# The input's part of the GRU gates: from two steps a product to a block a product

## The reference

```python
# x (16, 256, 512), initial state cond_2048 (16, 512), W_ih and W_hh (512, 1536)
def cell(h, x):
    gi = x @ W_ih + b_ih
    gh = h @ W_hh + b_hh
    i_r, i_z, i_n = jnp.split(gi, 3, axis=-1)
    h_r, h_z, h_n = jnp.split(gh, 3, axis=-1)
    r = jax.nn.sigmoid(i_r + h_r)
    z = jax.nn.sigmoid(i_z + h_z)
    n = jnp.tanh(i_n + r * h_n)
    h_new = (1.0 - z) * n + z * h
    return (h_new, h_new)
# hs: all 256 states; router: softmax of hs / |hs| @ router_w, the best two of eight, renormalised
for e in range(8):
    out = out + combine[:, e, None] * (hs @ Wa[e] @ Wb[e])     # ranks 128
return x + out
```

## Time and profile before

| | us |
|---|---|
| median of 3 runs (lowest, highest) | 1058.17 (1055.62, 1063.12) |
| the profiled execution | 1050.81 |
| its span, first to last instruction | 1048.9 |
| PE busy | 1001.5 |
| DVE busy | 856.9 |
| ACT busy | 722.4 |
| POOL busy | 298.0 |
| TensorE's granted clock, share of full speed | 0.995 |

### The profile page before, as it was taken

One profiled execution on the slowest core, in us unless ns is written; L12 is line 12 of the kernel. 1 busy time (PEld: TensorE's weight loads), 2 busy tenths in 40 slices (PEclk: granted clock), 3 DMA queues, 4 the chain that ended last, 5 costly groups with the idle time before them and its releaser, 6 DMA issues.

```text
span 1048.9 us, 71107 instructions
## 1 busy us (share of the span) xinstructions
PE 1001.5 (95%) x30225; PEld 860.6 (82%) x30225; DVE 856.9 (82%) x3215; ACT 722.4 (69%) x2824; POOL 298.0 (28%) x762
## 2 busy tenths in 40 slices
PE   4779999999999999999999999999999999999997
PEld 3678888888888888888888888878888888888874
DVE  6888888887887887888888888878888888788886
ACT  7677666776766776766667767767766767676663
POOL 2033223322232322232322233332223332222223
PEclk9899999999999999999999999999999999999999
DMA  8230111111111111111111111111111111110001
GB/s 289 88 90 20 29 30 32 26 31 29 30 32 29 25 32 30 30 31 29 29 28 29 30 32 32 27 28 30 28 33 33 28 28 33 27 29 20 14 5 32
DMA packets 49537, 39.48 MB, mean 38 GB/s; under 512 B 34676, under 2 KB 39112, under 8 KB 49224
## 3 DMA queue, kind: packets, MB, share of 16 engines
q1 hardware_dynamic: 48376, 31.41, 11.3%
q10 hardware_dynamic: 848, 3.54, 1.0%
HBM read 18.94 MB, written 8.39 MB: 26 GB/s over the span
## 4 chain that ended last, share of the span: by engine, by line
PE 90%; DVE 4%; issue 2%; ACT 2%; DMA 1%; ACTq 0%; DVEq 0%
PE obank L1043 16%; PE pairs L898 15%; PE gates L971 13%; PE gates L976 10%; PE nbank L1032 8%; PE ybank L1032 8%; PE nbank L925 7%; PE gates L988 5%; PE gates L984 5%; DMA wih<-in_L_cond_W_ih 1%; PE ybank L1010 1%; DVE tr L777 1%; DVE pre L780 1%; ACT nn L637 1%; DVE pre L786 0%
## 5 line engine op out<-in xcount | busy, mean ns | idle before, releaser
L1043 PE MATMUL obank<-wb,y 128*32 128x512 f16 (+1 forms) x2559 | 209.7, 380 | 4.6 <-issue 4.3
L898 PE MATMUL pairs<-wx,xs 128*32 128x256 f16 x6144 | 195.4, 273 | 5.3 <-issue 5.2
L465 POOL TENSOR_TENSOR y<-y 128x128 f16<-128x128 f32 x256 | 112.1, 438 | 306.6 <-ACT y L673 196.7
L777 DVE STREAM_TRANSPOSE tr<-gates 128x256 f32<-128x256 f32 x256 | 115.0, 449 | 76.9 <-PE gates L976 76.2
L971 PE MATMUL gates<-whh,st 128*32 128x256 f16 x4080 | 163.4, 275 | 14.4 <-DVE st L803 14.2
L629 ACT ACTIVATE rr<-pre 128x64 f32<-128x64 f32 x256 | 65.7, 257 | 158.8 <-DVE pre L780 158.3
L898 PEld LDWEIGHTS pairs<-wx,xs 128*32 128x32 f16 x6144 | 159.4, 97 | 12.0 <-issue 9.0
L976 PE MATMUL gates<-whh,hparts 128*32 128x256 f16 x4080 | 161.3, 273 | 0.4 <-issue 0.3
L971 PEld LDWEIGHTS gates<-whh,st 128*32 128x32 f16 x4080 | 96.6, 96 | 64.3 <-issue 47.1
L830 DVE SCALAR_TENSOR_TENSOR acc<-obank,comb,acc 128x512 f32<-128x512 f32 x186 | 138.4, 744 | 5.3 <-PE obank L1043 4.6
L1043 PEld LDWEIGHTS obank<-wb,y 128*32 128x32 f16 (+1 forms) x2559 | 82.8, 97 | 60.0 <-issue 12.1
(11 more groups left out here) (130 smaller groups left out, 1858.0 us busy)
## 6 DMA issues: line engine op xcount, KB each, us to landing
out<-outb SPq DMA_DIRECT2D x63, 128.0 KB
xin<-in_x SPq DMA_DIRECT2D x58, 128.0 KB
wih<-in_L_cond_W_ih ACTq DMA_DIRECT2D x4, 768.0 KB, 7.6
whh<-in_L_cond_W_hh SPq DMA_DIRECT2D x4, 768.0 KB, 12.1
wih<-in_L_ffn_Wb SPq DMA_DIRECT2D x8, 256.0 KB, 2.7
xs<-xh SPq DMA_TRANSPOSE x116, 3.2
wih<-in_L_ffn_Wa SPq DMA_DIRECT2D x4, 256.0 KB, 4.5
whh<-in_L_ffn_Wa SPq DMA_DIRECT2D x4, 256.0 KB, 3.6
```

The costliest lines, as they stand in the source:

```text
L465: nc.gpsimd.tensor_tensor(y[:, m % YB, 1, :], y32[:, :], y[:, m % YB, 0, :], ALU.subtract).then_inc(ylo_ready, 1)
L777: nc.vector.transpose(tr[:, 0:2 * K, :].rearrange("p (g k) c -> p g k c", k=K), g[:, 0:2 * P].rearrange("p (g c k) -> p g k c", g=2, k=K)) ...
L898: mm = nc.tensor.matmul(bank[32 * j:32 * j + 32, P:3 * P], turned(b, k, ph)[:, t0:t0 + 2 * B], wx[:, pw, k, j, :], start=False, stop=(k == ...
L1043: mm = nc.tensor.matmul(o_at(m)[rows * j:rows * j + rows, :], y[:, m % YB, ph, rows * j:rows * j + rows], wb[:, pw, m % NE, :], start=(ter ...
```

## The change

The input's part of r and z is computed for a whole block: its 128 rows are stationary in four tiles of 32 columns, `wx` of two column groups is moved, 512 columns a matmul, 12 terms for each of two halves (24 x 4 matmuls a block, a quarter of them on each even step, one block ahead). The product has its rows by step: partition 16t + b is step t of the block. `copy_gates` on ACT copies a half to SBUF (`gate_rows`), and `move_gates` on SP moves, for each step, the 16 rows of each of the four column groups by a small DMA (16 rows of 256 f32, 1 KB a row) to the rows 32j to 32j+15 of one of four slots `gate_in`. The rows 32j+16 to 32j+31 of these slots hold the biases, written once by POOL (`bias_gates`), so `seed` and `seed_z` copy a slot as it stands, and the sum of the two halves of rows adds them. The first block stays as it was, in pairs. `put_biases` is left at n = 0 and 2 alone. The last transposing DMA of a block has a semaphore of its own, so that the first part of the gates can begin with three of the four.

```diff
         gi_n = sb("gi_n", [P, 2, K, P])
+        GS, GZ = 4, 4
+        at_gs = 2 * NE * R
+        at_gz = at_gs + GS * D
+        gate_rows = hh_place[:, at_gs:at_gz].rearrange("p (i n) -> p i n", i=GS)
+        gate_in = hh_place[:, at_gz:at_gz + GZ * 3 * P].rearrange("p (i n) -> p i n", i=GZ)
...
@@ -161,6 +171,10 @@
         def n_at(b, m):
             return (gates[1], obanks[1], nbank, obanks[0])[m] if b == 0 else nbank
+        def gates_at(b, half):
+            return (obanks[1], ybank)[half] if b == 1 else pairs[half]
         def z_at(n):
             return gates[(n + 1) % 2][:, 2 * P:3 * P]
...
+            def move_gates(n):
+                b, t0 = n // S, n % S * B
+                sp.wait_ge(gates_copied, 2 * b)
+                sp.wait_ge(gates_biased, min(GZ, n - S + 1))
+                sp.wait_ge(seeded, n - GZ + 1)
+                sp.wait_ge(z_seeded, n - GZ + 1)
+                for j in range(K):
+                    sp.dma_start(gate_in[32 * j:32 * j + B, n % GZ, P:3 * P],
+                                 gate_rows[t0:t0 + B, (2 * (b - 1) + j // 2) % GS, j % 2 * 2 * P:(j % 2 + 1) * 2 * P]
+                                 ).then_inc(gates_moved[n % GZ], 16)
             def store(f, half):
                 sp.wait_ge(acc_done, (f + 1) * NE)
...
@@ -354,13 +386,16 @@
                     load_late(LEAD + n)
                 if n in (1, 2):
                     load_x(FIRST, n - 1)
+                if S <= n + 3 < T:
+                    move_gates(n + 3)
                 if 1 <= i and i + 2 < NB:
                     b = i + 2
                     if s == 0:
...
@@ -508,10 +543,20 @@
                 nc.gpsimd.tensor_scalar(bias_n_scaled[:, :], bias_n[:, :], PROD_SCALE, None, ALU.mult
                                         ).then_inc(bias_n_ready, 1)
+            def bias_gates(i, n):
+                pool.wait_ge(bias_kept, 1)
+                pool.wait_ge(weights_split, splits_before(N_GRU_SPLITS))
+                pool.wait_ge(both_parts_ready, 2 * (n + 2))
+                nc.gpsimd.tensor_scalar(gate_in[:, i, :], bias_sums[:, :], step_rows[:, 1:2], None, ALU.mult
+                                        ).then_inc(gates_biased, 1)
             prepare_state()
             def beside(n):
                 i, s = n // S, n % S
+                if n < GZ:
+                    bias_gates(n, n)
                 if s == 1 and 1 <= i:
                     fold_squares(i - 1, n)
...
+                    act.wait_ge(pair_done, n // 2 + 1)
+                else:
+                    act.wait_ge(gates_moved[n % GZ], 64 * ((n - S) // GZ + 1))
                 wait(act, rh_turned, n - 1)
                 wait(act, z_turned, n - 2)
@@ -586,30 +634,51 @@
                     act.wait_ge(gi_ready, 1)
                     act.wait_ge(z_turned, 1)
-                nc.scalar.activation(gates[n % 2][:, 0:2 * P], pairs[n // 2 % 2][:, 0:2 * P], ACT.Copy,
-                                     scale=step_rows[:, q:q + 1]).then_inc(seeded, 1)
+                if n < S:
+                    nc.scalar.activation(gates[n % 2][:, 0:2 * P], pairs[n // 2 % 2][:, 0:2 * P], ACT.Copy,
+                                         scale=step_rows[:, n % 2:n % 2 + 1]).then_inc(seeded, 1)
+                else:
+                    nc.scalar.activation(gates[n % 2][:, 0:2 * P], gate_in[:, n % GZ, 0:2 * P], ACT.Copy
+                                         ).then_inc(seeded, 1)
             def seed_z(n):
-                q = n % 2
-                act.wait_ge(pair_done, n // 2 + 1)
+                if n < S:
+                    act.wait_ge(pair_done, n // 2 + 1)
+                else:
+                    act.wait_ge(gates_moved[n % GZ], 64 * ((n - S) // GZ + 1))
                 wait(act, rh_turned, n)
                 wait(act, z_turned, n - 1)
                 if n == 0:
                     act.wait_ge(gi_ready, 1)
-                nc.scalar.activation(z_at(n), pairs[n // 2 % 2][:, 2 * P:3 * P], ACT.Copy,
-                                     scale=step_rows[:, q:q + 1]).then_inc(z_seeded, 1)
+                if n < S:
+                    nc.scalar.activation(z_at(n), pairs[n // 2 % 2][:, 2 * P:3 * P], ACT.Copy,
+                                         scale=step_rows[:, n % 2:n % 2 + 1]).then_inc(z_seeded, 1)
+                else:
+                    nc.scalar.activation(z_at(n), gate_in[:, n % GZ, 2 * P:3 * P], ACT.Copy).then_inc(z_seeded, 1)
+            def copy_gates(b, half):
+                i = 2 * (b - 1) + half
+                act.wait_ge(gates_done, i + 1)
+                if i == 0:
+                    act.wait_ge(weights_split, splits_before(N_GRU_SPLITS))
+                if i >= GS:
+                    for q in range(GZ):
+                        act.wait_ge(gates_moved[q], 64 * S // GZ * (b - GS // 2))
+                nc.scalar.activation(gate_rows[:, i % GS, :], gates_at(b, half)[:, :], ACT.Copy).then_inc(gates_copied, 1)
             def keep_biases():
                 act.wait_ge(bias_done, 1)
-                nc.scalar.activation(bias_sums[:, :], pairs[1][:, P:3 * P], ACT.Copy).then_inc(bias_kept, 1)
+                nc.scalar.activation(bias_sums[:, :], pairs[1][:, 0:3 * P], ACT.Copy).then_inc(bias_kept, 1)
             def put_biases(p):
                 act.wait_ge(z_seeded, 2 * (p - 1))
-                nc.scalar.activation(pairs[p % 2][:, P:3 * P], bias_sums[:, :], ACT.Copy).then_inc(bias_put, 1)
+                nc.scalar.activation(pairs[p % 2][:, P:3 * P], bias_sums[:, P:3 * P], ACT.Copy).then_inc(bias_put, 1)
             def add_gi_bias(b, m):
                 act.wait_ge(gi_done, K * b + m + 1)
...
@@ -684,8 +753,10 @@
                     read_router(i - 1)
                 if 0 <= n - SPLIT:
                     split_y(n - SPLIT)
-                if s % 2 == 0 and n + 4 < T:
+                if n in (0, 2):
                     put_biases(n // 2 + 2)
+                if s in (3, 4) and i + 1 < NB:
+                    copy_gates(i + 1, s - 3)
                 if s % 2 and i + 1 < NB:
                     add_gi_bias(i + 1, s // 2)
                 if s == 0 and 1 <= i:
...
@@ -901,6 +977,32 @@
                 if K - 1 in ks:
                     mm.then_inc(pair_done, 1)
+            def gate_part(b, half, ks, tiles):
+                rows = P // tiles
+                wait_turned(b)
+                if K - 1 in ks:
+                    wait_rest_turned(b)
+                if b == 1:
+                    pe.wait_ge(gi_ready, 2)
+                elif b == 2:
+                    pe.wait_ge(seeded, S // 2 + 2 * half + 2)
+                    pe.wait_ge(z_seeded, S // 2 + 2 * half + 2)
+                else:
+                    pe.wait_ge(gates_copied, 2 * (b - 2) + half + 1)
+                for k in ks:
+                    for ph, pw in TERMS:
+                        for j in range(tiles):
+                            mm = nc.tensor.matmul(gates_at(b, half)[rows * j:rows * j + rows, :],
+                                                  turned(b, k, ph)[:, rows * j:rows * j + rows],
+                                                  wx[:, pw, k, 2 * half:2 * half + 2, :].rearrange("p j c -> p (j c)"),
+                                                  start=(k == 0 and (ph, pw) == TERMS[0]),
+                                                  stop=(k == K - 1 and (ph, pw) == TERMS[-1]), skip_group_check=True)
+                if K - 1 in ks:
+                    mm.then_inc(gates_done, 1)
             def put_first_biases():
...
@@ -1078,17 +1186,25 @@
                     expert_down(n - DOWN)
                 if i + 1 < NB:
                     n_part(i + 1, s // 2, n)
+                if n in (1, 3):
+                    gate_part(1, n // 2, (0, 1), 1)
                 if s == 3 and 1 <= i:
                     route(i - 1)
                 if 0 <= n - DOWN:
                     expert_down(n - DOWN + 1)
             def beside_even(n):
+                i, s = n // S, n % S
                 if n == 0:
                     pair_part(1, (2, 3))
                     turn_first(2)
-                elif n + 2 < T:
+                elif n + 2 < S:
                     pair_part(n // 2 + 1, range(K))
+                    gate_part(1, n // 4, (2, 3), K)
+                b, part = (i + 2, 0) if s == 6 else (i + 1, s // 2 + 1)
+                if n >= 6 and b < NB:
+                    gate_part(b, part // 2, (2, 3) if part % 2 else (0, 1), K)
                 if 0 <= n - ADD:
                     up_ready(n - ADD)
                     for term in range(3):
...
```

More of the change, by code:

```diff
@@ L201, in gru_moe_kernel @@
         x_turned = [sem(f"x{i}_turned") for i in range(2)]
+        x_rest_turned = [sem(f"x{i}_rest_turned") for i in range(2)]
+        gates_done = sem("gates_done")
+        gates_copied = sem("gates_copied")
+        gates_biased = sem("gates_biased")
+        gates_moved = [sem(f"gates{i}_moved") for i in range(GZ)]
         pair_done = sem("pair_done")
@@ L1052, in up_ready @@
```

(2 more changed lines are left out.)

24 lines of the change are left out of this document (15 added, 9 removed).

## The result

The changed kernel takes 1098.49 us (median of 4 runs, 1095.14 to 1102.78) against 1058.04 for the kernel before on the same chip: ratio 1.038, 95% interval 1.032 to 1.044. It is 40 us slower; the forecast was 19 us faster, and the range ended at 1060. The profiled execution took 1096.05 us, its span 1094.3, at a granted clock of 0.996.

What follows compares the result with a forecast made beforehand. TensorE and the recurrence were taken as nearly balanced, with instruction-fetch stalls on top. Span 1048.9 - 16 (stalls) - 1 (columns) + 0.5 = 1032.4 us, 1034 with 1.9 around; two thirds of the median's 7.4 excess gave 1039; range 1026 to 1060.

Steps and rivals of the forecast that it cites:

- The step that failed: SP's four small DMAs a step: 0.43 us each to issue, 1.72 a step, landing 3.2 us, no cost in time.
- that cover: Lead of SP's moves over ACT's need: two steps or 7.4 us; worst step takes 6.3, 1.1 ahead of need.
- Rival 2: Moves landing later than 4.8 us delay ACT's seed once a block; up to 56 us lost, 1095 us; chance 0.09.
- The stalls: TensorE waiting for its next instruction packet, some 25 us; fewer matmuls leave 9, gain 16, bounds 3 and 23.
- Rival 3: Nothing left of TensorE's instruction stalls: 23 us gained, 1030 to 1033 us; chance 0.15.
- Rival 1: TensorE's fetch stalls stay, perhaps refills slowed by the 992 small DMAs; 1051 to 1062 us, middle 1057; chance 0.18.
- The columns: TensorE's gate part of 24 matmuls takes 1.30 to 1.37 us, against 1.31 before; 1 us gained in all.
- The reading of the floor: The recurrence sets at least 3.71 us a step; a step with full TensorE work lies 0.06 us above it.
- ACT: Copies of 0.64 us replace bias work of 0.40; seeds at 0.40 against 0.43; nothing taken as gain or loss.
- First block: Block 1's gate parts added to steps 1 to 4; together with the last block's dropped pairs part, +0.5 us.
- the signs it named for being wrong: ACT's seeds waiting for gate_in's landing, "issue" waits at 20 us or more, or unstalled even steps over 3.85 us.

Runs made afterwards that it cites:

- e1: The changed kernel with none of the small DMAs issued, seeds waiting once for the biases (gates incomplete); 1026.61 us, ratio 0.970 to the kernel before.
- e3: The changed kernel with two of the four small DMAs a step (column groups 0 and 2; gates incomplete); 1027.12 us, ratio 0.971.
- e5: The changed kernel with three of the four small DMAs a step (column groups 0 to 2; gates incomplete); 1026.69 us, ratio 0.975.
- e2: As e1, but each gate part is 48 matmuls of 256 columns in place of 24 of 512; 1057.44 us, ratio 1.002.
- e11: As e10, complete, but each gate term is one matmul of 128 stationary columns in place of four in column groups; 1053.61 us, ratio 0.994.
- e10: The changed kernel, complete, with gates moved through memory by 10 DMAs a block for 32, gate parts one even step earlier; 1049.24 us, ratio 0.988.
- e12: As e10, complete, with gate parts reordered so those needing the last slices come later, and POOL's bias fills spread over steps 0 to 6; 1029.70 us, ratio 0.980.
- e8: As e7, complete, but each gate term is one matmul of 128 stationary columns in place of four of 32; 1075.39 us, ratio 1.022.
- e7: The changed kernel, complete, with each small DMA moving two steps' 32 rows and POOL adding the biases in the slot; 1079.21 us, ratio 1.025.

## Why the prediction was wrong, point by point

**The step that failed** is that of the moves: "Such an issue (16 rows, four column groups) takes 0.43 us on SP, so 1.72 a step. SP is only a queue here: in its fullest ordinary step it adds a transposing DMA, 1.17, 2.9 of 3.7 us.", and from it "The move costs nothing while that cover lasts." Two things were wrong in it.

- *The size.* 0.43 us was the issue of a load from memory, and of rows of 512 bytes, so not "the same shape" as the moves' 1 KB. The moves, from SBUF to SBUF, take 0.59 in the median and 0.68 in the mean, and four in a row take 2.41 to 3.62 us in the timeline above, not 1.72. The text bounded the landing by two rows and the issue by none.
- *The sum.* The steps were judged one by one and never added over a block. In my own numbers the block was 32 x 0.43 + 4 x 1.17 + loads and stores, about 20.8 us of 30.4: room enough. Even with the moves' median and transposes of 1.25 it would be 26.4. What fills the queue is the means with their tails (21.56 us of moves and 5.88 of transposes a block) and 2.84 us of short gaps, a term that the sum had at nothing: 32.75 in all against the 30.5 to 30.6 that a block takes in e1, e3 and e5. There is no room left, and then no cover of two steps helps, since a queue that is too slow on average eats any lead. It is the throughput of the issuing engine, not the latency of one transfer, that decided.

**Rival 2**, moves that come late, gave 1095 us, nearly the time measured, by another mechanism; the agreement is a coincidence. It put the price on the landing, from 4.8 us on, once a block at s = 0. The landing was 2.3, and the steps that lose are s = 3 to 6, with x beside the moves. Its 0.09 was too low since it looked at the wrong quantity. e3 and e5 tell the two apart: a late landing would not mend itself by leaving out one of four moves whose landing doesn't change.

**The stalls.** The mechanism held (each of the longer stalls ends at a fixed distance behind an instruction packet, see e2), the term was too small: 16 us with an upper bound of 23, against 31 measured (e1 against e2) and 25 to 30 (e5 and e3 against the kernel before). Rival 3, nothing left of them, was right in that, though its 23 us was low too. The assumed exponential with mean 0.6 left 0.36 of the stalls; in e1 the like waits come to 3.1 us, of 25.8 before. Such waits account for some 25 of the 31 us (28.3 us in e2, counted like the 3.1 of e1); the rest presumably stands ahead of lines whose waits for the state cover it, and was not tested. Rival 1, that they stay, and with it the small DMAs slowing the fetches, is out: with all 992 of them the changed kernel has 5.8 us of such waits.

**The columns.** 1.30 to 1.37 us a part were given, 1.29 measured; even steps without a wait are at 3.71 to 3.72, odd ones at 3.77. The reading of the floor stands.

**ACT.** The seeds take 0.378 us, less than the 0.40 assumed, the copies 0.60 for 0.64, and nothing came of them on the path in e3 and e5. **First block.** From step 1 to step 9 it is 30.47 us before, 30.57 in the changed kernel, 30.74 in e1 and 30.21 in e5: a term of 0.5 us can't be told from this scatter.

So without the moves, by its own terms, the prediction would have been right in sign and 12 us too careful: 1039 against 1027. Of the signs it named for being wrong, "if ACT's seeds waited for the landing of gate_in" is what came.

## What to carry to other kernels

Sum the issue time of every DMA on a queue over a whole period of the kernel, with the duration of the same kind of DMA (source, destination) or, where the trace has none, with bounds, and the gaps between issues, before asking whether one of them lands in time; near the period the cost has a knee and not a slope. When small transfers must rearrange rows, buy fewer and larger ones, even by way of memory, and look what is queued behind them. Halving the number of matmuls at equal columns can be worth more than its column time says, where the trace shows "issue" waits of weight loads in the midst of dense groups.

## What the runs showed of the hardware that I had not expected

- SP's time to issue a DMA differs from one DMA to the next, and more rows did not make it longer: SBUF to SBUF 0.59 us in the median for 16 rows as for 32, 0.51 at the least and up to 1.94; from memory, 16 partitions of 4 KB, 0.43; half a block of x, 64 rows of 2 KB, 0.63; 128 rows to memory 0.35; transposing 1.25. POOL issued the first kind in 0.50. Why they differ, and where the tail comes from, was not tested.
- 744 of these moves cost at most some us and 992 cost some 70 of 1027.
- 256 columns in place of 512 at equal work cost 31 us, 25 of them seen as "issue" waits of up to 1.4 us each, which end 1.2 to 1.6 us behind the landing of an instruction packet.
- A POOL add that starts with DVE's makes the latter 0.88 us in place of 0.30; a sum that starts during the add ends 0.15 us after it (62 of 63).
- One matmul of 128 stationary columns in place of four of 32 wasn't free. In e11 the up-products behind such a part begin later. Timeline of PE and of PEld:

```profile
507.91 1.47 PE L1013 MATMUL pairs<-wx,xs 128*128 128x512 f16 x6
509.31 1.26 PE L1164 MATMUL obank<-wb,y 128*32 128x512 f16 x20
```

```profile
509.30 0.77 PEld L1164 LDWEIGHTS obank<-wb,y 128*32 128x32 f16 x20 [0.42 <-issue]
```

  From the part's start to the next is 1.40 us where four tiles take 1.30, and even steps are 3.93 us in the median where e10 has 3.77 and e12 3.72. e8, whose even steps DVE's late sums held at 4.13, took 4 us less than e7 with the same edit, e11 took 4 more than e10. What holds the weight loads after a 128-column one was not tested.
